# Attention scores and value spread in groups of four row tiles over four PSUM banks, the third attention one turn later, a written order for each engine

## What is computed

```python
x = L0(ctx, x)   # 16 heads; keys and values from ctx and x together (256 tokens), int mask;
                 # then rmsnorm and an MLP 256 -> 1024 -> 256 with gelu
x = L1(x, ctx)   # 32 query heads over 8 key heads of 8 channels, additive mask, layer norm
x = L2(x, ctx)   # RWKV block: token shift, five mixes, decay; per head
                 #   out_t = r_t (bonus * k_t v_t + s);  s = k_t v_t + w_t * s
                 # group norm, gate, output; then a channel mix
x = L3(x, ctx)   # 16 heads over layer-normed ctx, bool mask; x + tanh(gate) * out
```

## Time and profile before

| | |
|---|---|
| median of 3 runs | 1259.38 us (1259.19 to 1260.45) |
| the profiled execution | 1264.44 us |
| its span, first to last instruction | 1262.5 us |
| TensorE, VectorE, ScalarE, GpSimd busy | 1127.0, 956.6, 651.5, 261.0 us |
| mean granted TensorE clock | 0.945 of full speed |

### The profile page before, as it was taken

The page is one execution under the profiler, slowest core; times in us unless marked ns, Lnnn a source line. Parts: engine busy times, 40 slices in busy tenths (PEclk is TensorE's granted clock), DMA queues, the critical chain, the costliest instruction groups (busy, mean ns, idle before and its releaser), DMA issues. The chain is left out here.

```text
span 1262.5 us, 24184 instructions
## 1 busy us (share of the span) xinstructions
PE 1127.0 (89%) x7776; PEld 765.1 (61%) x7776; DVE 956.6 (76%) x3401; ACT 651.5 (52%) x2483; POOL 261.0 (21%) x349
## 2 busy tenths in 40 slices
PE   5878899999999998999999998999999998897656
PEld 4564666665665666666666666666666666554434
DVE  2707697789967998789968998689968998675834
ACT  1528343784448553774448553674438553582024
POOL 3210223102410214102420214102321214101310
PEclk9788899999999999999999999999999999898858
DMA  8000000000000000000000000000000000000000
GB/s 296 2 9 20 1 2 1 22 2 15 2 21 2 16 1 1 22 2 16 1 22 2 12 5 1 22 2 15 1 22 2 6 11 1 1 2 11 1 1 9
DMA packets 18092, 18.91 MB, mean 15 GB/s; under 512 B 7216, under 2 KB 16432, under 8 KB 17712
## 3 DMA queue, kind: packets, MB, share of 16 engines
q1 hardware_dynamic: 17968, 17.37, 4.6%
HBM read 15.27 MB, written 2.10 MB: 14 GB/s over the span
## 5 line engine op out<-in xcount | busy, mean ns | idle before, releaser
L831 ACT ACTIVATE E<-S,nmax 128x128 f32<-128x128 f32 (+1 forms) x1024 | 424.1, 416 | 229.4 <-DVE nmax L1020 215.1
L1020 DVE CUSTOM_DVE_ANT_0 S<-psS,mb 128x128 f32<-128x128 f32 (+1 forms) x1024 | 264.3, 320 | 87.7 <-PE psS L534 64.4
L494 PE MATMUL ring<-slot,w_l 128*128 128x256 f32 x992 | 251.5, 400 | 14.0 <-DVE slot L1202 5.2
L494 PEld LDWEIGHTS ring<-slot,w_l 128*128 128x128 f32 x992 | 188.8, 198 | 60.0 <-issue 12.8
L548 PEld LDWEIGHTS psT<-ident,E 128*128 128x128 f32 x1280 | 146.2, 147 | 128.1 <-ACT E L831 73.3
L534 PE MATMUL psS<-keys,slot 32*128 32x512 f32 (+1 forms) x768 | 194.4, 581 | 30.1 <-DVE nmax L1020 19.0
L1035 DVE COPY ET<-psT 128x512 f32<-128x512 f32 x320 | 206.2, 681 | 7.8 <-PE psT L548 7.8
L548 PE MATMUL psT<-ident,E 128*128 128x128 f32 x1280 | 203.8, 293 | 7.8 <-DVE ET L1035 3.2
L831 ACT ACTIVATION_READ_ACCUMULATOR E<-S,nmax 128x1 f32 x1024 | 191.6, 187 | 0.0
L504 PE MATMUL ring<-w_l,slot 128*128 128x256 f32 (+1 forms) x640 | 151.9, 384 | 7.7 <-DVE slot L1051 5.8
L504 PEld LDWEIGHTS ring<-w_l,slot 128*128 128x128 f32 x640 | 115.3, 194 | 36.6 <-issue 10.7
(11 more groups left out here) (119 smaller groups left out, 1183.3 us busy)
## 6 DMA issues: line engine op xcount, KB each, us to landing
slot<-in_ctx SPq DMA_DIRECT2D x8, 256.0 KB, 2.7
slot<-in_x SPq DMA_DIRECT2D x8, 256.0 KB, 2.7
w_l<-in_wl SPq DMA_DIRECT2D x1, 2048.0 KB, 11.2
out<-slot SPq DMA_DIRECT2D x8, 256.0 KB, 2.1
w_l<-in_wl SPq DMA_DIRECT2D x2, 768.0 KB, 7.1
w_l<-in_wl SPq DMA_DIRECT2D x1, 1152.0 KB, 9.9
m0i<-in_m SPq DMA_DIRECT2D x8, 128.0 KB, 3.2
mb<-in_m SPq DMA_DIRECT2D x8, 128.0 KB, 2.8
```

Of the source, the lines that this page charges most:

```text
L494: m = pe.matmul(b[:, a, :], w[:, k, m0 + a * P:m0 + (a + 1) * P], src[:, k, :], start=(k == 0), stop=(k == kt - 1))
L831: ins = act.activation(E[:, g % RING_E, h * w:(h + 1) * w], S[:, g % RING_S, h * w:(h + 1) * w], ACT.Exp, bias=nmax[:, g % 4, h:h + 1], sc ...
L1020: ins = dve.tensor_tensor_reduce(S[:, g % RING_S, h * w:(h + 1) * w], psS[g % 2][:, h * w:(h + 1) * w], bias[:, bb, :], -1.0, HUGE, ALU.ad ...
```

## The change

- `scores` is called for four jobs at a time, and writes four banks `psS`, one from each strip of 32 rows. `mask` reads them; `S` has four buffers.
- `spread_v` is called twice a turn (`vp0`, `vp1`) instead of eight times. Each call is eight matmuls of 32 rows by 256 columns, strip r writing bank r of `psS`. The steps `vr0` to `vr7` stay on VectorE and GpSimd and read `psS`. `gather` is called twice instead of four times, with the same matmuls.
- The two banks `psT` are gone. The 40 transposed tiles of a turn become products of the ring of three banks. All are emptied by VectorE, as before.
- The third attention (scores to o3) leaves the back for a stream of its own, one turn later; its keys and values (k3, v3) go from the front to the back. The phases are start, first, second, steady five times, closing, last, end.
- In place of `SCHEDULE` there is an order for each of four engines, over all phases.
- `V0`, `V1`, `V3` hold each head once in a field of 32 columns, and `window` picks 32 columns with the head at its place; values take one VectorE instruction instead of four.
- Weight reordering on GpSimd moves from ahead of phase first to behind `x1T` in it. OUT and X4 get buffers of their own; SP sends the output ahead of the next input loads.

```diff
-BANKS = 3
-RING_K, RING_S, RING_E = 2, 2, 2
+QUAD = 4
+BANKS = 3
+RING_K, RING_S, RING_E, RING_Z = 2, 4, 2, 4
-SCHEDULE = [
-    "mask0", "xaT", *jobs(0, 0, 2), "shift1", *jobs(0, 2, 3), "cols", *jobs(0, 3, 4), "t", *jobs(0, 4, 8), "mw",
...
+PE_ORDER = """
+@start xT cT q0 @first aT @start k0l k0c v0c v0l k1 v1 @first scores0.0 turn0.0 scores0.4 turn0.1 turn0.2 weigh0.1
...
-    xf=(0, 0, 5), seed=(0, 0, 8), scan=(0, 0, 8), z=(0, 0, 8), gathered=(0, 0, 8), first_token=(0, 0, 2),
+    **{n: (0, 0, 8, 0) for n in ("seed", "spread", "kv", "scan", "z", "gathered")},
...
-        psS = [st.enter_context(nc.psum_tensor(f"psS{n}", [P, 512], F32)) for n in range(2)]
-        psT = [st.enter_context(nc.psum_tensor(f"psT{n}", [P, 4, P], F32)) for n in range(2)]
+        psS = [st.enter_context(nc.psum_tensor(f"psS{n}", [P, 512], F32)) for n in range(QUAD)]
...
                     for x, bb in enumerate(bbs):
-                        for m in (n, n + 1):
+                        for m in range(n, n + QUAD):
                             t, _, rt = attention_jobs(layer)[m]
...
-                            ins = pe.matmul(psS[(first_job[layer] + m) % 2][:, x * w:(x + 1) * w], queries,
+                            ins = pe.matmul(psS[m % QUAD][:, x * w:(x + 1) * w], queries,
                                             keys[rows, group % RING_K, x * w:(x + 1) * w], start=True, stop=True)
...
-                    if g >= 2:
-                        pe.wait_ge(sems["copied"], turn("copied", g - 1))
-                    elif phase != "first":
-                        pe.wait_ge(sems["copied"], before("copied"))
+                    b = start(("turn", layer, n)).rearrange("p a (h s) -> p (a h) s", h=2)
                     for k in range(4):
-                        m = pe.transpose(psT[g % 2][:, k, :], E[:, g % RING_E, k * P:(k + 1) * P], ident[:, :])
-                    m.then_inc(sems["turned"], 1)
+                        m = pe.transpose(b[:, k, :], E[:, g % RING_E, k * P:(k + 1) * P], ident[:, :])
+                    m.then_inc(sems["product"], 1)
...
-                def spread_v(u):
-
-                    ct, j = u // 4, 2 * (u % 4)
-                    b = start(f"vr{u}")
+                def spread_v(ct):
+
+                    if ct == 1:
+                        pe.wait_ge(sems["kv"], turn("kv", 4))
+                    else:
+                        pe.wait_ge(sems["masked"], turn("masked", FIRST[phase].get(1)))
                     for a in range(2):
-                        m = pe.matmul(b[:, a, :], spread_j[:, j + a, :], vT[:, ct, :], start=True, stop=True)
-                    m.then_inc(sems["product"], 1)
+                        for r in range(4):
+                            rows = slice(32 * r, 32 * r + 32)
+                            m = pe.matmul(psS[r][:, a * T:(a + 1) * T], spread_j[rows, r + 4 * a, :], vT[rows, ct, :],
+                                          start=True, stop=True)
+                    m.then_inc(sems["spread"], 4)
...
-                    for half in range(2):
-                        for ct in range(CT):
-                            d = dst[:, :, half, ct * P:(ct + 1) * P]\
...
+                    d = dst[:, :, 16:].rearrange("p b (h x) -> p b h x", x=32)[:, :, :, 0:16]
+                    v = bank(phase, i, name).rearrange("p b (h d) -> p b h d", d=16)
```

More of the change, by code:

```diff
@@ L78 @@
[L78 to L88, removed]
+PARTS_OF_JOB = ("scores", "mask", "exps", "turn", "weigh")
@@ new lines, with order @@
+HAS = {"start": (0,), "first": (0, 1), "second": (0, 1, 2), "steady": (0, 1, 2, 3), "closing": (1, 2, 3), "last": (2, 3),
+       "end": (3,)}
+TIMES = {"start": 1, "first": 1, "second": 1, "steady": TURNS - 3, "closing": 1, "last": 1, "end": 1}
+PHASES = tuple(HAS)
+def order(text):
+    steps = []
+    for word in text.split():
+        if word[0] == "@":
+            phase, i = ("steady", int(word[7:])) if word[1:7] == "steady" else (word[1:], None)
+        elif "." in word:
+            name, n = word.split(".")
+            steps.append((phase, i, (name[:-1], int(name[-1]), int(n))))
+        elif word[:6] == "gather":
+            steps.append((phase, i, ("gather", int(word[6:]))))
+        else:
+            steps.append((phase, i, word))
+    return steps
@@ L451, in _ @@
             program("first", None)
-            for i in range(TURNS - 2):
+            program("second", None)
+            for i in range(TURNS - 3):
                 program("steady", i)
@@ L780, in program @@
                         token_major("o3", attnT, W3["o"])
-            program("start", None)
-            program("first", None)
-            pe.wait_ge(s_w2, 18 * 16)
-            pe.wait_ge(s_lanes, 2)
-            for i in range(TURNS - 2):
-                program("steady", i)
-            program("closing", None)
-            program("last", None)
+            program()
         @block.scalar
@@ L974, in _, with program @@
             dve.wait_ge(s_setup, 1)
-            def program(phase, i):
-                turn, before, product, left = counts(phase, i)
-                first_job = FIRST[phase]
+            def program():
                 def norm_stats(src, n):
@@ L1392, in inverse_root @@
                         .then_inc(sems[f"rstd{n}"], 1)
-                for step in steps_of(phase):
-                    if step[0] == "job":
+                for phase, i, step in ORDER["POOL"]:
+                    turn, before, product, left = counts(phase, i)
+                    earlier_left = counts(*phase_before(phase, i))[3] if phase != "start" else None
+                    if step[0] == "scores":
                         _, layer, n = step
-                        if n < NJ[layer] and n % KEYS_OF[layer] == 0:
+                        if n % KEYS_OF[layer] == 0:
                             group = FIRST_GROUP[phase][layer] + n // KEYS_OF[layer]
```

669 lines of the change are left out of this document (429 added, 240 removed).

## The result

The changed kernel takes **1162.16 us** (1159.75 to 1163.21, 4 runs), against 1259.91 in the same session: a ratio of 0.922, 95% interval 0.919 to 0.924. The forecast was 1127, the range 1088 to 1180. The span of the profiled execution is 1157.9 us; its own time, 1159.75, is the lowest of the four.

A forecast was written before the change was run, and what follows sets the result against it. TensorE was taken to bound the loop (94% of a 143.4 us turn), VectorE equally loaded after the change. Phases 26 + 106 + 118 + 645 + 122 + 83 + 30 = 1130, plus 1.9 less 5.1, gave 1127 us; range 1088 to 1180.

The forecast's parts named there:

- Quads and spread: TensorE's scores in fours at 1.06 us a quad save 10.6 us a turn; spread visits at 1.2 us save 5.4.
- strips rival: Four strips overlap no more than two: quads 2.12 us, spreads 2.1, turn 142, total some 1220; chance 0.07.
- TensorE 118.9 us a turn: TensorE's work in a steady turn: 134.9 us less 16.0 saved by scores in fours and spread.
- VectorE 118.3: VectorE's work in a steady turn: 119.5 us less 1.2 for fewer value instructions.
- The turn of 129: Steady turn: TensorE's 118.9 us plus 10 us of its idle, 129 us; turns of 126 to 133 had chance 0.55.
- Order changes on SP cost nothing: SP's output ahead of loads is free, the loads being covered by a turn, with DMA busy 3%.
- 129 less 11: Phase second: a steady turn without third attention, 11 us less, 118 us.
- with a steady turn's idle share: Phase closing: TensorE 124.4 us less 16, VectorE 111, plus a steady turn's share of idle, 122 us.
- The ends: Outer phases: start 26, first 106, last 83 (third attention fits its gaps at price 0), end 30 us.
- Both at 96%: Rival: both engines stay 96% busy in the steady turn, turn 124 us, total 1093; chance 0.17.
- Masks hold up the ring: Rival: VectorE's masks delay emptying the ring, 8 us a turn, turn 137, total 1182; chance 0.16.
- Ring of three banks slower: Rival: 89 products a turn wait on three banks; at 0.35 us each, turn 150, total about 1280; chance 0.05.

The follow-up runs named there:

- x_own: The changed kernel with X in a tile of its own, so its load waits for XB2 instead of XB1: 1159.48 us, ratio 0.917.
- relief: The changed kernel with the fifth mixed tile's add moved from VectorE to GpSimd and the mask's zeros set only once: 1161.69 us, ratio 0.921.
- copies_shared: The changed kernel with the copies of jobs 1, 5 and 9 of layer 0 (24 in all) moved from VectorE to ScalarE: 1169.70 us, ratio 0.928.
- e_ring4: The changed kernel with four buffers instead of two for the ring of exponentials: 1159.35 us, ratio 0.922.
- scalar_load: The changed kernel with one more 256-element ScalarE copy behind each of the 24 jobs a turn of layers 0 and 3: 1177.38 us, ratio 0.932.
- relief_x_e: The changed kernel with the edits of relief, x_own and e_ring4 together: 1157.81 us, ratio 0.918.
- pool_norm_first: The changed kernel with GpSimd doing the norm behind the second attention ahead of the next pair's sum0: 1168.66 us, ratio 0.927.
- load_only: The changed kernel with an extra 512-element VectorE sum in SBUF behind each of the 24 copies a turn of layers 0 and 3: 1257.56 us, ratio 0.997.
- copies_twice: The changed kernel with VectorE's 24 copies a turn of transposed banks in layers 0 and 3 done twice: 1271.45 us, ratio 1.006.

## Why the prediction was right, and what its 35 us of error are

**Quads and spread: right.** Taken at 1.06 (1.3 allowed in layer 3) and 1.2; measured 1.07, 1.08 in most of layer 3, and 1.08. L718 is busy 98.0 us where L534 had 194.4. The inference from three strips in the earlier trace rows to four held, and the strips rival is out. One sign was missed: at one spread TensorE waited 6.3 us for VectorE (L787 <- kv L1424, in the row "last"), where no wait beyond 1 us was forecast.

**TensorE 118.9 us a turn: right** (118.2). **VectorE 118.3: too high by 4.8.** The 1.2 us for the values were right, though not by the sum given for them (0.4 three times and 0.8 are 2.0, not 1.5): VectorE's instructions on V are busy 18.8 us instead of 27.7, 1.1 a turn. The step that failed is the unspoken one behind "119.5 less 1.2", that all the rest keeps its length. VectorE's total fell by 37.7 us, so 28.8 of it, 3.6 a turn, without an edit to the instructions. The scan has 7.4 of this (96.9 us instead of 104.3) and the normalisation 7.5 (28.3 instead of 35.8). Here the reason can be read: they meet GpSimd's instructions less. Of the 128 scan instructions 47 overlap one, before 69; these took 1.01 us on average in both kernels, the others 0.67 and 0.68. Of the 64 normalisations 18 overlap one (0.68 us each), before 23 (0.94), and the others took 0.41 in both.

**The turn of 129: nearly right, 130.5.** The idle of TensorE was put at 10 us and is 11.7 in the turn shown. Over five turns that is 7.3 us. The reasoning holds: two engines of nearly equal load do not come together at 96%. The load runs show it from the other side, since more work on either engine lengthens the turn, by 0.6 to 1.1 us per us within it.

**"Order changes on SP cost nothing: the loads are covered by a turn": wrong as a reading, small as a term.** X shares its tile with X1, so its load starts only when GpSimd has read X1. In the turn shown TensorE waits 2.42 us for it, and in four of the turns 8.5 in all:

```profile
463.00 1.10 PE L668 MATMUL ring<-ident,slot 128*128 128x128 f32 x8 [2.42 <-DMA slot<-in_x]
```

x_own takes the wait away and leaves the steady turn as it was (131.0), because TensorE's next product waits for the group norm; the 2.7 us of its median are not clear of noise. So the misreading cost next to nothing.

**Second, 118 forecast, 126.5 measured: the step "129 less 11".** TensorE's work fell by 7.0 us against a steady turn (118.2 to 111.2), not by 11, and its idle rose from 11.7 to 15.3. A part of the 4 us is where the cut lies: the row has 856 records, 116 fewer than the mean steady turn, though a third attention has 152 (the last row). The rest is that removed work was priced at one to one, while the turn gave back less. What the added idle hangs on was not tested.

**Closing, 122 forecast, 129.9 measured: the step "with a steady turn's idle share".** TensorE has as many records as before (903, 900), but took 113.7 us and not 124.4 less 16, at clock 0.93 instead of 0.96, and idled 16.2. The step's own numbers give 118 us by TensorE and 121 by VectorE. Much of the rest is the clock: over this row, cut the same way, relief and copies_shared took 125.1 us at 0.97, e_ring4 126.3 at 0.95, x_own and scalar_load 128.3 and 128.5 at 0.95 and 0.96, relief_x_e and pool_norm_first 129.8 and 130.4 at 0.92 and 0.91. So some 5 of the 7.9 us go with a clock that fell further here than in other executions of nearly the same program. Why it fell is open.

**The ends: right in the numbers, in part by luck.** Start and first 134.2 (132), last 82.8 (83), end 32.2 (30). But the first row holds six jobs of the next pair that the forecast did not put there (and first's own terms add to 14 us, where 12 was taken off). And "last" was to take in a third attention at a price of 0, while seven of its eight copies lie in the row before. That price was not tested. Without that work the row is 1.0 us shorter than before (83.8), so the 5 us that the spread might save there do not show either.

The sum of these is 2.2 + 8.5 + 7.3 + 7.9 - 0.2 + 2.2 = 27.9 us of span. The other 7.5, but for rounding, come from the last step: the profiled execution before was 5.1 us above its median, this one is 2.4 below.

**The rivals.** *Both at 96%* fell: the shortest steady turn is 127.5. *Masks hold up the ring* was to show in waits for the copies of ET at the transpositions. There TensorE waited for them once, 1.4 us, against 31.9 for the exponentials. At other lines it waited 16.5 us for ET at L763 and 7.8 at L886 in the whole run, 3 a turn, and 7.9 us for masks (L718), where the rival gave 8 a turn. *Ring of three banks slower* fell. The Trainium skill's rule ("TensorEngine Tiling (Array Packing)", section PSUM Bottleneck) was half right here: after the change VectorE, which does the copies, is a bound in layers 0 and 3 (load_only, copies_twice), but giving 24 of the 320 copies to ScalarE cost 8.6 us.

## What to carry to other kernels

When one engine sheds enough work that a second has the same load, add up the busier engine stretch by stretch, between points where one must wait for the other, not over the whole turn: here the rows at 95 to 97% belong to two engines by turns. A wait that the profile lists is worth only the distance to the next wait behind it in the same queue (8.5 us taken away in x_own, no gain shown). Work taken out of a turn can give back less than its length: TensorE shed 16.3 us of a turn (134.9 to 118.6 on average), and the turn became 12.9 shorter. When rows of two orders are compared between the same cuts, count what lies in them first: here some fell right because work had moved across a cut.

## What the runs showed of the hardware that was not expected

- Four strips of 32 rows took as long as two: 16 records of 256 columns in 1.08 us (0.98 once), 8 of 512 columns in 1.07, start to start. The next group, in the 128-row form, started within the time of a pair, so no cost of the change of form was visible.
- A VectorE instruction of 0.407 us from SBUF to SBUF (the normalisation) took up to 1.50 us where GpSimd's instructions ran beside it, and a scan of 0.68 us took 1.01 on average. So GpSimd's order changes VectorE's load.
- With more load on VectorE in layers 0 and 3, TensorE's granted clock over the run was lower: 0.901 to 0.914 in the ten executions of load_only, 0.948 to 0.953 in the four of the changed kernel. TensorE was busy 41.7 us longer with the same 7776 records.
